# Squares of two blocks taken from ScalarE to VectorE in the run-up of an attention and feed-forward kernel

## What is computed

```python
q = _l2norm(proj(Wq))                     # 16 heads of 16 features
k = _l2norm(proj(Wk))
v = proj(Wv)
attn = jnp.einsum('bhqd,bhkd->bhqk', q, k)
mask = (rel < 0) | (rel >= WINDOW)        # WINDOW = 128
bias = jnp.where(mask[None, :, :], jnp.asarray(NEG_INF, x.dtype), alibi)
attn = jax.nn.softmax(attn + bias[None], axis=-1)
out = jnp.einsum('bhqk,bhkd->bhqd', attn, v)
...
x = _layernorm(x + attention(x))
h = jax.nn.gelu(jnp.einsum('bsd,hd->bsh', x, bw1) + b1, approximate=False)
out = jnp.einsum('bsh,dh->bsd', h, bw2) + b2   # bw = mean(|w|) * sign(w)
x = _layernorm(x + out)
```

## Time and profile before

| | us |
|---|---|
| median of 3 runs | 370.71 |
| lowest and highest | 370.42 and 370.77 |
| profiled execution | 370.34 |
| its span, first to last instruction | 368.5 |
| busy: TensorE | 354.0 (96%) |
| busy: VectorE | 324.2 (88%) |
| busy: ScalarE | 309.8 (84%) |
| busy: GpSimd | 273.2 (74%) |

### The profile page before, as it was taken

The page is one execution under the profiler, slowest core; times in us unless marked ns, Lnnn a source line. Parts: engine busy times, 40 slices in busy tenths (PEclk is TensorE's granted clock), DMA queues, the critical chain, the costliest instruction groups (busy, mean ns, idle before and its releaser), DMA issues. The chain is left out here.

```text
span 368.5 us, 13120 instructions
## 1 busy us (share of the span) xinstructions
PE 354.0 (96%) x4445; PEld 244.5 (66%) x4445; DVE 324.2 (88%) x857; ACT 309.8 (84%) x539; POOL 273.2 (74%) x418
## 2 busy tenths in 40 slices
PE   8799999999999999999999999999999999999991
PEld 6555676667767766776776667775666766766771
DVE  5978899898898898998889998869789999999995
ACT  2598898888898898898899999988888888887873
POOL 1189999889989999999999999756564664764321
PEclk9999999999999999999999999999999999999997
DMA  7668854844654655768766773303303413403113
GB/s 237 135 127 188 176 117 89 171 85 113 137 120 90 139 116 112 158 146 166 146 168 144 154 135 64 59 4 59 59 0 59 115 43 74 115 30 85 59 60 114
DMA packets 106885, 40.20 MB, mean 109 GB/s; under 512 B 92128, under 2 KB 105824, under 8 KB 106720
## 3 DMA queue, kind: packets, MB, share of 16 engines
q1 hardware_dynamic: 106848, 39.73, 48.5%
HBM read 12.72 MB, written 4.19 MB: 46 GB/s over the span
## 5 line engine op out<-in xcount | busy, mean ns | idle before, releaser
L1385 POOL TENSOR_SCALAR_AFFINE_SELECT prob<-prob 128x512 f32<-128x512 f32 x252 | 153.0, 642 | 11.3 <-ACT prob L692 11.2
L692 ACT ACTIVATE prob<-ps 128x1024 f32<-128x1024 f32 (+1 forms) x128 | 122.1, 1008 | 12.9 <-PE ps L388 12.9
L549 PE MATMUL ps<-yT,sgn 128*128 128x512 f16 x256 | 61.1, 379 | 0.0
L764 ACT ACTIVATE ps<-ps,bias,alpha 128x512 f32<-128x512 f32 x64 | 47.8, 750 | 15.8 <-PE ps L549 12.7
L419 PE MATMUL ps<-wqkv,xt 128*128 128x512 f32 x124 | 58.7, 596 | 1.4 <-DVE qkn L955 1.1
L1453 POOL TENSOR_TENSOR resid<-z,resid 128x256 f32 (+1 forms) x31 | 22.6, 730 | 46.1 <-DVE z L1182 46.1
L409 PE MATMUL ps<-prob,vdiag 128*17 128x128 f32 x1024 | 51.3, 274 | 0.2
L409 PE MATMUL ps<-prob,vnext 128*17 128x128 f32 x992 | 49.9, 273 | 0.0
L549 PEld LDWEIGHTS ps<-yT,sgn 128*128 128x128 f16 x256 | 25.0, 98 | 22.6
L452 PE MATMUL ps<-wo,oT 128*128 128x256 f32 x128 | 36.1, 404 | 0.1
L388 PE MATMUL ps<-qkT 64*64 64x192 f16 (+2 forms) x1024 | 33.8, 248 | 2.0 <-DMA qkT<-parts 1.4
(11 more groups left out here) (116 smaller groups left out, 684.8 us busy)
## 6 DMA issues: line engine op xcount, KB each, us to landing
xt<-in_xT SPq DMA_DIRECT2D x32, 128.0 KB, 2.1
resid<-in_x SPq DMA_DIRECT2D x32, 128.0 KB, 2.2
out_dram<-resid SPq DMA_DIRECT2D x7, 512.0 KB, 2.9
w<-in_w2T SPq DMA_DIRECT2D x1, 1024.0 KB, 8.2
w<-in_w1T SPq DMA_DIRECT2D x4, 256.0 KB, 3.3
w_nat<-in_w SPq DMA_DIRECT2D x4, 256.0 KB, 3.5
wqkv<-in_wqkvT SPq DMA_DIRECT2D x3, 256.0 KB, 3.7
qkT<-parts SPq DMA_TRANSPOSE x39, 4.3
```

The source lines that it names most:

```text
L549: mm = nc.tensor.matmul(ps[:, bank, :], sgn1[:, c, P * k:P * k + P], yT[:, par, a, c, :, :], start=(m == 0), stop=(m == 2 * DC - 1))
L692: nc.scalar.activation(to, scored, ACT.Exp, scale=QK_SCALE ** -2).then_inc(exp_done, 1)
L764: nc.scalar.activation(bank, bank, ACT.Gelu, bias=bias1[:, k:k + 1], scale=alpha1[:, k:k + 1]).then_inc(gelu_done, 1)
L1385: return nc.gpsimd.affine_select(out=at, in_=at, compare_op=ALU.is_ge, fill=0.0, base=-near, pattern=[[0, CH], [1 if near else -1, P]], ch ...
```

## The change

The squares of blocks 4 and 5 are made by VectorE. ScalarE's steps 1 and 2 no longer contain them (`squared=False`), and its high halves stand behind the first two exponentials as in the loop's steps. VectorE makes each square with two instructions from the same PSUM bank: the bank times 1/`QK_SCALE`² into `sq`, then the bank times `sq` into `sq`. A new semaphore `own_scaled` holds the second until the first is done; the sums then wait for the second as before. Both stand directly behind `normalise_rows` of the block before, the sums and the seed directly behind them. `fade_values(2, 2)` and the second piece of |w2| stand behind the sums now. The number of instructions grows by four on VectorE and falls by two on ScalarE; TensorE's order is the same.

```diff
-        zlast_sum, rows_by_act, last_row = sem("zlast_sum"), sem("rows_by_act"), sem("last_row")
+        own_scaled, zlast_sum, rows_by_act, last_row = sem("own_scaled"), sem("zlast_sum"), sem("rows_by_act"), sem("last_row")
...
-                     squares_first=False, before_rows=None, amid=None, tail=None):
+                     squares_first=False, squared=True, before_rows=None, amid=None, tail=None):
...
-                if next3:
+                if next3 and squared:
                     squares(i + 3, 1 - par)
...
-            step(1, 1, strips=False, ln=False, squares_first=True)
-            step(2, 2, strips=False, ln=False, squares_first=True)
+            step(1, 1, strips=False, ln=False, squared=False)
+            step(2, 2, strips=False, ln=False, squared=False)
             step(3, 3, ln=False, squares_first=True)
...
+            def own_squares(n, par):
+
+                dve.wait_ge(qkproj_done, n + 1)
+                dve.wait_ge(ss_done, n)
+                nc.vector.tensor_scalar(sq[:], ps[:, QK[par], :], 1.0 / QK_SCALE ** 2, None,
+                                        ALU.mult).then_inc(own_scaled, 1)
+                dve.wait_ge(own_scaled, n - 3)
+                nc.vector.tensor_tensor(sq[:], ps[:, QK[par], :], sq[:], ALU.mult).then_inc(sq_done, 1)
...
             round_of(0, True, False)
             normalise_rows(3, 1)
+            own_squares(4, 0)
+            sums_of(4, False)
             fade_values(2, 2)
-            sums_of(4, False)
             double(3, 1)
             round_of(1, True, False)
             normalise_rows(4, 0)
+            own_squares(5, 1)
+            sums_of(5, False)
             abs_w2(P, P + P // 2)
-            sums_of(5, False)
             double(4, 0)
```

## The result

| | before | after |
|---|---|---|
| median | 370.74 | 371.95 |
| lowest and highest | 369.58 and 370.79 | 371.01 and 373.22 |
| runs | 6 | 6 |
| profiled execution | 370.34 | 371.01 |
| its span | 368.5 | 369.3 |

The changed kernel is slower, by a ratio of 1.0042 (95% interval 1.0027 to 1.0058). The difference of the two profiled executions, 0.67 us, is smaller than that of the medians, 1.21, and the trace tells why: the execution after starts better. TensorE's first products took 2.10 us where they had taken 2.31, and began 0.21 earlier, so VectorE's rows of block 3 start at 23.12 instead of 23.54, before anything of the change has run. From here on every time is therefore a distance from the start of these rows. TensorE turned the rows of block 0 12.82 us behind them before (36.36 - 23.54) and 13.97 after (37.09 - 23.12): +1.15 us.

A forecast was written before the change was run, and what follows sets the result against it. TensorE, full in the loop, keeps any run-up lateness: 2.88 us of new VectorE work less two holes gives 0.64, held seeds and copies the rest; +1.15 makes 371.5 profiled, 371.9 median; range 370.8 to 372.7.

The forecast's parts named there:

- Price of the new instructions: VectorE, blocks 4 and 5: scaled copy and product taken as 0.69 us each, with 0.03 us between dependent ones.
- ScalarE's gain of 0: ScalarE, steps 1 and 2: dropping two squares of 0.60 us gains 0, since high halves wait for VectorE's rows.
- The first hole of TensorE: Run-up, TensorE's wait ahead of the strips of block 0: grows by 0.90 us, strips starting at 34.29.
- The held seeds: VectorE, blocks 4 and 5: seeds fall into GpSimd's subtractions and end with them, at 27.18 and 33.86.
- The first rival: Run-up: seeds slip through; if block 5's is not held, +0.54 us, 371.25; chance 0.15.
- The sum: Run-up: new instructions less holes 0.64 us, held seeds and copies the rest to 1.17; total +1.15 us.
- the two holes: VectorE's waits of 1.11 and 1.13 us ahead of its copies in `double`, which the new instructions fill.
- What the loop keeps: Loop behind the run-up: all four engines leave step 3 1.1 to 1.17 us late, and that stays.
- The second rival: Steps 6 and 7: TensorE's waits there absorb the delay, leaving +0.1 to +0.4 us, 370.9; chance 0.12.
- the fifth: Run-up: longer holes lower TensorE's clock to 1.2 GHz, costing over 3 us more; chance 0.02.
- the prediction's other reason: Behind the run-up: VectorE and GpSimd are shifted alike with TensorE, 1.1 against 1.17 us, so its waits stand.

The follow-up runs named there:

- both_do_it: Changed kernel, but ScalarE keeps all squares while VectorE also makes those of blocks 4 and 5 into an unread spare tile; 372.19 us, ratio 1.0051.
- no_squares: Changed kernel without VectorE's scaled copies and products, so nobody squares blocks 4 and 5; 371.39 us, ratio 1.0028 to the kernel before.
- no_seed_late: Kernel before, without VectorE's seed step from block 6 on (ScalarE halves squares, sums negated into `half`); 368.90 us, ratio 0.9947; run again 369.32, 0.9954.
- seed_by_sum: Changed kernel with the seed step of blocks 4 and 5 as a small negated sum instead of a TENSOR_SCALAR; 371.18 us, ratio 1.0004 to before.
- after_again: Changed kernel run once more without an edit; 372.25 us, ratio 1.0032 to the kernel before.

## Why the prediction was right

Its steps, with 0.42 us added to the times of the changed kernel, because its rows of block 3 started that much earlier:

| step | forecast | measured + 0.42 |
|---|---|---|
| seed of block 4, start and end | 26.31, 27.18 | 26.31, 27.17 |
| copy of block 3, end | 28.46 | 28.45 |
| rows of block 4, start | 30.21 | 30.20 |
| high halves of block 4, start | 30.93 | 30.92 |
| seed of block 5, start and end | 32.98, 33.86 | 32.96, 33.83 |
| strips of block 0, start | 34.29 | 34.27 |
| copy of block 4, end | 35.13 | 35.11 |
| rows of block 0 turned | 37.53 | 37.51 |

Every step of this table came out to within 0.03 us. That the median came out within 0.05 us of the forecast 371.9 is in part luck: like kernels differ by some tenths there, and the two profiled executions differ by 0.67 us only.

- **Price of the new instructions.** Taken as 0.69 us each with 0.03 between; measured 0.68 and 0.69, 0.72 from start to start. The 731 ns of the earlier trace rows, a write of 16-bit values, was the wrong neighbour, and the right one was the product of the earlier trace rows.
- **ScalarE's gain of 0.** `both_do_it` and `no_squares` both show it, to 0.01 us. In step 2 it was a near tie, though: in the kernel before ScalarE came from its square 0.49 us behind 29.86, at 30.35, just when VectorE's rows allowed the high halves. In `no_seed_late`, where the projection came 0.35 us later, the square did hold the high halves, and with them the run-up. In such an execution the change would give something back; no trace of the changed kernel has one.
- **The first hole of TensorE.** The forecast had it grow by 0.90 us ahead of the strips. The 0.90 us are there, but 0.55 of them are a wait for the exponentials ahead of the scores, which the forecast did not name; the turned strips came 0.87 us later. The high halves of block 5 came 1.06 us later, where 1.1 to 1.17 had been said.
- **The held seeds.** `seed_by_sum` shows it by form alone. The first rival (seeds that slip through) had priced them too low: it gave +0.54 us for the seed of block 5 alone slipping, and with both seeds out of the way the loss was not 0.5 but 0, since block 4's part goes as well.
- **The sum.** Its total is right and its split is not. It charged 0.64 us to the new instructions (2.88 less the two holes) and the rest to the held seeds and the copies. `seed_by_sum` has the same 2.88 us of new instructions and loses 0.02 us, so all of the loss hangs on the held seeds. VectorE had room beyond the two holes: the copy of block 4 starts 0.22 us later there than before and lasts 0.50 instead of 0.70 us, so it ends as before. By blocks the whole is 0.56 + 0.58. That they add is no law: both lose about one turn of GpSimd's cuts, 0.60 us.
- **What the loop keeps.** +1.15 at the turned rows, +1.09 at the strips of block 6, +1.07 at block 23, +0.88 at block 31. `after_again` keeps 1.12, 1.15 and 1.17. The second rival's absorption is 0.06 us up to block 6, what the 1.1 against 1.17 us had allowed; the further 0.19 us between block 23 and block 31 lies within the 0.3 us by which like kernels differ there. And the clock of the fifth stayed at 1.00:

```profile
33.20:41.30 8.10, 6.58 (x106) 4.11 (x106) 7.03 (x16) 6.81 (x14) 7.31 (x12) 1.00 0.88 202
```

- **One reason that does not hold.** The prediction said that in a loop where TensorE is busy 152.95 of 153.20 us nothing on the other engines costs time unless it reaches TensorE, and that TensorE has no room there in which to catch up. The run-up's loss did pass through, but `no_seed_late` takes 128.43 us from the strips of block 5 to those of block 23, where the kernel before takes 129.17, with TensorE as busy in both:

```profile
71.85 0.60 PE L436 MATMUL ps<-id,strips 128*128 128x128 f32 x4
201.02 0.60 PE L436 MATMUL ps<-id,strips 128*128 128x128 f32 x4
69.80:198.00 128.20, 128.17 (x2028) 1.00 0.62 131
```

```profile
71.77 0.60 PE L436 MATMUL ps<-id,strips 128*128 128x128 f32 x4
200.20 0.60 PE L436 MATMUL ps<-id,strips 128*128 128x128 f32 x4
69.80:198.00 128.20, 128.11 (x2054) 1.00 0.63 132
```

The distances between the two rows of strips are 129.17 and 128.43 us for the same work. TensorE is recorded busy for 128.17 and 128.11 of 128.20 us, so most of the 0.74 us that the second saves was recorded as work in the first. The room shows in the rows of its weight loads. Four steps of the stretch, one in every four, take 7.22 to 7.23 us before and 7.08 to 7.09 in `no_seed_late`, from strips to strips. In the first of them, which starts with the strips of block 6 (78.94 and 78.86), the load of VectorE's `otok` for the turned rows reads, before and in `no_seed_late`:

```profile
80.96 0.28 PEld L443 LDWEIGHTS ps<-id,otok 128*128 128x128 f32 x2 [0.53 <-DVE otok L886]
```

```profile
80.69 0.14 PEld L443 LDWEIGHTS ps<-id,otok 128*128 128x128 f32 x1 [0.34 <-DVE otok L891]
```

So TensorE's loads did wait for VectorE in the loop, 0.19 us longer in the longer step, while its product rows read full. The profile page says that the ends of matrix products are modelled, and this is what it means: a full share of PE is not proof of an engine without room. The steps 6 and 7 lie ahead of this stretch, 7.66 and 7.88 us from strips to strips before and 7.08 and 7.89 in `no_seed_late`; of their waits for `otok` only the longest shows in a product row, the 0.27 us at 66.56. That the run-up's loss passed through the loop therefore rests on the prediction's other reason, that all engines were shifted alike, and not on a TensorE without room; this is argued, no run tests it.

## What to carry to other kernels

Before work goes to an engine with holes, look at the small instructions behind it: if they are a TENSOR_SCALAR from and to SBUF (or one of the Newton steps with two SBUF inputs, 0.55 to 0.61 us beside the cuts, 0.18 and 0.19 at 15.79 to 16.42 in the kernel before, where GpSimd stood still), and the work moves them under a GpSimd instruction, they can cost more than the work itself. Here each held seed cost 0.57 us, and the 1.44 us of work ahead of it nothing. Try first to fold such a step into a neighbour (a factor in a scale, a sum written negated), or give it a form that is not held; that is worth a try even where nothing has been moved. Read TensorE's weight loads beside its products before you call it full. Compare executions by the distance between two instructions behind the start, not by the span, when the effect is under 1 us.

## What was not expected

- The start of an execution moves. TensorE's first products took 2.39 and 3.11 us in the two executions of `no_seed_late`, and 2.31 and 2.10 us in the traces before and after; the transfer of block 2 kept TensorE waiting 0.60 and 1.37 us in two executions of one program. Behind block 23 they differ again, but little of that stays: the next step from strips to strips was 7.57 us before, 7.09 after and 7.58 in `after_again`, and from block 23 to block 31 it was 51.20, 51.01 and 51.22 us.
- A loop whose TensorE was recorded full became 0.74 us shorter when a step of VectorE was taken out.
